# Routing the second layer in two groups of token tiles, with a memory region per expert, and splitting all its weights during the attention

## The reference: two layers of graph attention and experts over 1354 nodes

```
x = x + adj @ (layernorm(x) * W)                                   # layer 0, graph
h = layernorm(x); a = h + attention(layernorm(h), 8 heads)         # layer 0, block
x = x + a + moe0(layernorm(a))      # top 2 of 8 experts, the first 271 tokens of each
f = layernorm(x) @ Wg               # layer 1, graph
a1 = f @ attn_l; a2 = f @ attn_r
w = exp(leaky_relu(a1 + a2.T) - rowmax) * adj
x = x + elu((w / w.sum(1)) @ f)
t = layernorm(x)                    # layer 1, experts: no capacity limit
p = softmax(t @ Wg2 + bg); mask = top 2 of 8
x = x + sum_e (p * mask)[:, e] * (gelu(t @ W1[e] + b1[e]) @ W2[e] + b2[e])
```

## Time and profile before

| what | value |
|---|---|
| time, median of 3 runs | 944.22 us (939.36 to 947.76) |
| the profiled execution's own time | 947.76 us |
| its span, first to last instruction | 946.0 us |
| mean granted TensorE clock | 0.903 |
| busy: PE, DVE, ACT, POOL | 780.6, 599.7, 407.8, 313.5 us |
| fill of the scatter region of layer 1 (before) | 3842.5 KB in one transfer |
| split of the weights | 32 loads and 64 writes of 512 KB |

### The profile page before, as it was taken

The page is one execution under the profiler, slowest core; times in us unless marked ns, Lnnn a source line. Parts: engine busy times, 40 slices in busy tenths (PEclk is TensorE's granted clock), DMA queues, the critical chain, the costliest instruction groups (busy, mean ns, idle before and its releaser), DMA issues.

```text
span 946.0 us, 13697 instructions
## 1 busy us (share of the span) xinstructions
PE 780.6 (83%) x4168; PEld 591.3 (63%) x4169; DVE 599.7 (63%) x1174; ACT 407.8 (43%) x841; POOL 313.5 (33%) x329
## 2 busy tenths in 40 slices
PE   3978899999999998508799956599653999999993
PEld 3976555555555434407799954487532788888882
DVE  5665777766666756628888926696551565666662
ACT  3215435555556464504376633541500545444451
POOL 2000256666666761086400012000064223233221
PEclk9988979999999999757799987799656999999997
DMA  7698767787877662036544336450832168772223
GB/s 254 208 286 314 197 229 229 229 278 253 248 244 246 211 221 74 1 134 217 199 166 173 125 128 260 192 182 1 353 120 95 21 166 266 223 212 42 37 29 76
DMA packets 67217, 168.79 MB, mean 178 GB/s; under 512 B 20382, under 2 KB 45110, under 8 KB 64192
## 3 DMA queue, kind: packets, MB, share of 16 engines
q1 hardware_dynamic: 45664, 105.01, 33.5%
q0 software_dynamic: 21504, 63.17, 22.0%
HBM read 104.33 MB, written 58.90 MB: 173 GB/s over the span
## 4 chain that ended last, share of the span: by engine, by line
PE 71%; DVE 11%; issue 7%; DMA 4%; ACT 3%; POOL 2%; SPq 0%; POOLq 0%; DVEq 0%; ACTq 0%
PE ps L1182 11%; PE ps L1162 7%; PE ps L1174 5%; PE ps L1477 5%; PE ps L1393 4%; PE ps L1455 4%; PE ps L1288 3%; PE ps L1290 3%; PE ps L1289 3%; PE ps L1457 3%; PE ps L1456 3%; PE ps L1479 3%; PE ps L1464 3%; PE ps L1135 2%; DVE mx L1632 2%
## 5 line engine op out<-in xcount | busy, mean ns | idle before, releaser
L1632 DVE TENSOR_REDUCE mx<-ps 128x1 f32<-128x452 f32 x264 | 148.2, 622 | 66.0 <-PE ps L1162 65.1
L891 ACT ACTIVATE expo<-ps 128x452 f32<-128x452 f32 x264 | 124.5, 552 | 92.2 <-PE ps L1174 91.3
L1182 PE MATMUL ps<-expo,v_st 128*64 128x452 f32 (+1 forms) x576 | 117.7, 531 | 0.0
L1162 PE MATMUL ps<-k_st,q_st 96*128 96x452 f32 x264 | 106.7, 418 | 5.1 <-DVE mx L1632 4.7
L1056 ACT ACTIVATE h<-ps,b_l 128x128 f32<-128x128 f32 x232 | 63.0, 383 | 100.4 <-PE ps L1464 98.1
L1174 PE MATMUL ps<-q_st,k_st 98*128 98x452 f32 x264 | 96.8, 390 | 2.2 <-ACT expo L891 2.0
L828 POOL DMA_INDIRECT sum_d<-y1t,goal x29 | 46.3, 1596 | 140.3 <-DVE share L1975 113.8
L1477 PE MATMUL ps<-w_ring,h_hi 128*128 x232 | 83.1, 396 | 2.8 <-DVE y1t L2002 2.8
L1162 PEld LDWEIGHTS ps<-k_st,q_st 96*128 96x128 f32 x264 | 51.0, 193 | 52.2 <-DVE mx L1632 35.9
L1993 DVE COPY h1pre<-ps 128x1024 f32<-128x1024 f32 x29 | 35.5, 1225 | 72.7 <-PE ps L1457 72.7
L767 POOL TENSOR_TENSOR part_lo<-part,part_hi 128x512 fp32r<-128x512 f32 x56 | 70.8, 1290 | 0.4
(11 more groups left out here) (294 smaller groups left out, 1789.4 us busy)
## 6 DMA issues: line engine op xcount, KB each, us to landing
w_l<-w_l SPq DMA_DIRECT2D x8, 2053.0 KB, 8.7
part<-w_l POOLq DMA_DIRECT2D x32, 512.0 KB, 5.3
w_split_d<-part_lo POOLq DMA_DIRECT2D x32, 512.0 KB, 3.9
adj<-adj_t SPq DMA_DIRECT2D x22, 704.0 KB, 4.5
w_split_d<-part_hi POOLq DMA_DIRECT2D x28, 512.0 KB, 3.6
w_ring<-w_split_d SPq DMA_DIRECT2D x8, 1365.5 KB, 7.3
w_ring<-w_split_d SPq DMA_DIRECT2D x4, 1365.0 KB, 5.8
xs_d<-zeros SPq DMA_DIRECT2D x1, 3842.5 KB, 26.8
```

The lines of the kernel that those rows point to most:

```text
L891: act.activation(expo[g % 8][:, :], ps[:, 3 + g % 3, 0:QC], ACT.Exp, scale=SCALE).then_inc(s_exp, 1)
L1162: pe.matmul(ps[:, i % 3, 0:KC], q_st[h % 3][0:3 * DK, (n // KB) * P:(n // KB + 1) * P], k_st[h % 3][0:3 * DK, (n % KB) * KC:(n % KB + 1) * ...
L1182: return pe.matmul(ps[at:at + 2 * DK, 6 + g // T % 2, lo:hi], v_st[h % 2][:, kt, :], expo[g % 8][:, lo:hi], start=kt < 2, stop=kt == T - 1 ...
L1632: dve.tensor_reduce(mx4[:, n // KB, n % KB:n % KB + 1], ps[:, i % 3, 0:KC], AX_X, ALU.max).then_inc(s_mx, 1)
```

## The change

Seven edits go together.

- **Region per expert.** `xs1_d` has E regions of NP = 1408 rows (1060 bytes each) and one spare tile. The row number is the position plus a constant (`C_OFF1`), and the expert stage finds a tile's rows by a table `tile_row`, loaded into a register by POOL.
- **Fill.** The fill of `xs1_d` in the first stage shrinks to 128 rows; instead SP fills one expert's region (1408 rows) in each head.
- **Split.** All 32 parts are split in the attention; `choose` of layer 0 waits for all of them. The four late parts among the experts of layer 0 are gone.
- **Two groups.** Layer 1 is routed for tiles 0 to 7 (`route1(2, ...)`), then for 8 to 10 (`route1(3, ...)`). PE makes the kept products of tiles 8 and 9, turns and routes tiles 0 to 7, and then makes tile 10's. POOL scatters 16 times for the first group, then 6 times.
- **Scores apart.** The 2 score columns have products of their own into one bank, for a whole group, ahead of the features; ACT copies them once per group. The features have 256 columns and three banks. The features of tiles 8 to 10 come after the maximum.
- **Turned rows.** ACT copies both halves in the graph of layer 1; DVE none.
- **Adjacency rows.** SP issues the first three loads after all gathers.

```diff
-SLOTS1 = TILES1 * P
+SLOTS1 = E * NP + P
+    c[:, C_OFF1:C_OFF1 + E] = np.arange(E) * NP + 1
 # SP
-            sp.dma_start(xs1_d.rearrange("(k p) d -> p k d", p=P),
-                         zeros[:, None, :].to_broadcast([P, TILES1, ROW])).then_inc(s_zfill, 16)
+            sp.dma_start(xs1_d[E * NP:SLOTS1, :], zeros[:, :]).then_inc(s_zfill, 16)
...
                     if h + 1 < H:
                         load_values((h + 1) % 2, h + 1)
+                sp.dma_start(xs1_d[h * NP:(h + 1) * NP, :].rearrange("(k p) d -> p k d", p=P),
+                             zeros[:, None, :].to_broadcast([P, T, ROW])).then_inc(s_zfill, 16)
                 store_third(h, 0)
...
             sp.wait_ge(s_y0_ps, PRIMED + E)
+            for t in range(T):
+                sp.wait_ge(s_gath[t], 16)
             for j in range(3):
                 sp.dma_start(adj1[j][:, :], adj[j]).then_inc(s_adj1[j], 16)
-
-            for t in range(T):
-                sp.wait_ge(s_gath[t], 16)
 # POOL
-            split_parts(0, EARLY, part_hi)
-            pool.wait_ge(s_zfill, 48)
+            for n in range(PARTS1):
...
+            pool.wait_ge(s_zfill, 48 + 16 * E)
...
-            split_parts(EARLY, PARTS1, part_hi_late)
...
-            pool.wait_ge(s_norm_act, normed_act(5))
-            for n in range(2):
-                pool.wait_ge(s_idx, 2 + n)
-                for t in range(T):
-                    pool.indirect_dma_start(...)
+            for lo, hi, done in ((0, GA, 1), (GA, T, 3)):
+                for n in range(2):
+                    pool.wait_ge(s_idx, done + n + 1)
+                    for t in range(lo, hi):
+                        if n == 0:
+                            pool.wait_ge(s_norm_act, normed_act(5, t))
+                        pool.indirect_dma_start(...)
...
-                pool.dma_start(x1t[t % 3][:, :], xs1_d[t * P:(t + 1) * P, :]).then_inc(s_x1l[t % 3], 16)
+                row = pool.value_load(tile_row[0:1, t:t + 1], min_val=0, max_val=E * NP)
+                pool.dma_start(x1t[t % 3][:, :], xs1_d[bass.ds(row, P), :]).then_inc(s_x1l[t % 3], 16)
+            pool.wait_ge(s_te, 1)
 # ACT, graph of layer 1
             normed_group(0)
             turned_group(0)
+            column_scores(0)
+            features(0, 2, 0)
             normed_group(1)
-            features(0, 2)
+            features(2, 4, 0)
             turned_group(1)
-            features(2, 4)
+            column_scores(1)
+            features(4, 6, 1)
             normed_group(2)
-            features(4, 6)
+            features(6, 8, 1)
             turned_group(2)
-            features(6, T)
+            column_scores(2)
             act.wait_ge(s_am, 3)
             act.activation(fg[:, 0, :], agap[:, :], ACT.Exp)
             act.activation(fg[:, 1, :], agap[:, :], ACT.Exp, scale=0.2).then_inc(s_fg, 1)
+            features(8, T, 2)
...
+            def routed_group(n, lo, hi):
...
+                root_table()
+                raw_copies(3, lo, hi)
+                root_group(8 + n, lo, hi)
+                act.wait_ge(s_lg, 2 + n)
+                act.activation(probs[:, lo:hi, :], lg[:, lo:hi, :], ACT.Exp).then_inc(s_pexp, 1)
+                act.wait_ge(s_g1b, GB)
+                for t in range(lo, hi):
+                    act.activation(sent[:, t, 0:D], x_res[:, t, :], ACT.Identity, ...)
 # PE
+            column_scores(0)
             features(0)
             turn_group(1)
+            column_scores(1)
             features(1)
             turn_group(2)
             spread(0)
-            features(2)
+            column_scores(2)
             spread(1)
             pe.wait_ge(s_am, 1)
             pe.transpose(ps[0:1, 1, 0:P], a_max[:, :], ident).then_inc(s_small, 1)
             spread(2)
             pe.wait_ge(s_am, 2)
             pe.matmul(ps[:, 1, P:P + 1], ones[0:1, :], a_max1[:, :], ...)
+            features(2)
...
+            pe.wait_ge(s_z, GB)
+            rest(0)
+            rest(1)
+            pe.wait_ge(s_z, GA)
+            routed(0, GA, 1)
+            rest(2)
+            positions(2, 0, GA, 7)
+            pe.wait_ge(s_lg, 2)
+            routed(GA, T, 2)
+            positions(3, GA, T, 3)
+            pe.wait_ge(s_idx, 5)
 # DVE
             for k in range(2):
-                dve.wait_ge(s_lo_out[k], 16 * (EARLY // 2))
-            choose(0)
+                dve.wait_ge(s_lo_out[k], 16 * (PARTS1 // 2))
+            choose(1, 0, T)
...
+            def route1(k, lo, hi, bank):
...
+                choose(k, lo, hi)
+                dve.wait_ge(s_g1b, GB)
+                ...                                   # probs, comb: 5 steps
+                dve.wait_ge(s_pos, k)
+                ...                                   # slot, sa, sb_: 5 steps
+                row_number(sa, 0, lo, hi)
+                row_number(sb_, 1, lo, hi)
             settle(0, (0, GA), (0, GA))
-            elu(0, 0, GA)
+            step(elu(0, 0, GA))
+            route1(2, 0, GA, 7)
             dve.wait_ge(s_g1b, GB)
             settle(1, (0, GB), (GA, T))
             step(elu(1, GA, T))
-            inverse_root(mv[:, :, 1], rstd)
-            choose(1)
+            route1(3, GA, T, 3)
...                                                   # then the tables, with tile_row
```

More of the change, by code:

```diff
@@ L318, in tr_act_before @@
         def tr_act_before(r):
-            return sum(TR_BY_TILE.get(m, 3) for m in range(r))
+            return sum(6 if m == BY_ACT_HALVES else TR_BY_TILE.get(m, 3) for m in range(r))
         def tr_dve_before(r):
-            return sum(0 if m in TR_BY_TILE else 3 for m in range(r))
+            return sum(0 if m in TR_BY_TILE or m == BY_ACT_HALVES else 3 for m in range(r))
         def scratch(name, shape):
@@ L1404, in _, with rest @@
                     graph1(i * 3 + (2 + k), (2 + k) % 3, False)
[L1405 to L1406 removed]
+            def rest(t):
                 for j in range(T):
```

295 lines of the change are left out of this document (150 added, 145 removed).

## The result

| | kernel before | kernel after |
|---|---|---|
| time, median of 4 runs beside each other | 945.99 us (939.36 to 952.47) | 958.66 us (957.85 to 959.49) |
| ratio, 95% interval | | 1.0151 [1.0101, 1.0201] |
| span of the profiled execution | 946.0 us | 957.2 us |

The forecast was 941.5 us, no difference that can be told, and its range ended at 957. Slower by over 1% had a chance of 0.22. The two profiled spans lie 11.2 us apart, the forecast had them at -2.9. So 14.1 us are to be found.

What follows compares the result with a forecast made beforehand. PE was taken as busy for most of the span, with gains only where it waits. The terms +19 - 15.5 + 1.9 - 8.3 = -2.9 us gave, against 944.22, a forecast of 941.5 us, range 927 to 957.

Steps and rivals of the forecast that it cites:

- step 1: Attention: eight fills at 2.7 us each and four added parts end the split at 411.4; layer 0's routing starts 19 us late.
- step 5: Routing of layer 1: two groups start the scatters sooner, the ring's load stays hidden, b2 becomes the bound; -8.3 us.
- The rule of shared engines: Split in the attention: all queues share 16 DMA engines, so each fill costs its full 3.9 us, 31 instead of 21.6.
- Step 2: Experts 0 and 1 of layer 0: without the late splits beside them their stalls go; -15.5 us, bounds -5 and -17.
- Rival C: Experts 0 and 1 are slow for the cold clock, not POOL; step 2 gives only 3, time 954; chance 0.08.
- The port between DVE and POOL: Out projection: DVE's two-input additions and POOL's splits block each other; split perhaps 2 us later, sum 2 us worse.
- Step 3: Gather of layer 1: first gathers no longer run beside adjacency loads; -2.2 us at the first normalized tile.
- Step 4: Turning and features of layer 1: longer score columns offset by savings, taken as 0; then +1.9 us for copies before the exponentials.
- The last stage: Stage after the routing of layer 1: counted at no change, 0 us.
- B: Attention: fills delay POOL's loads and low writes more, slower by 1% at 4.2 us each, 960 at 5; chance 0.20.
- A: Attention: fills hide in POOL's computing time, 1 us each or less; time 928, or 922 if free; chance 0.27.
- D: Routing of layer 1: the first group's scatters start no earlier, step 5 gives 0, time 949.5; chance 0.10.

Runs made afterwards that it cites:

- run 8: Run 3's kernel, its last four parts loaded and written back but computed by POOL in one column only; ratio 0.7% below run 3.
- run 1: Kernel after with its eight fills moved from the attention heads to beside the experts of layer 0; 946.50 us against 946.93 for the kernel before.
- run 5: Kernel before plus, in each head, a fill of 1408 rows of a separate region, 28 parts still in the attention; 0.34% slower.
- run 3: Kernel before with all 32 parts split in the attention, nothing else changed; ratio 1.0019.
- run 2: Kernel after with the last four parts split among the experts of layer 0 again, fills still in the attention; 954.59 us.
- run 12: Run 9 with 28 parts in the attention and the last four among the experts of layer 0; 937.55 us against 936.88 for run 9.
- run 7: Run 1 with the kept products of tiles 8 to 10 made before tiles 0 to 7 are turned; layer-1 routing stage 63.8 us, whole time not given.
- run 9: Kernel after with fills beside layer 0's experts, the old feature stage and kept products first; 936.88 us against 944.51 for the kernel before.
- run 6: Run 1 with turning, score columns and features of the layer-1 graph as in the kernel before; ratio 0.9954 against 1.0018 for run 1.
- run 10: Run 1 with ACT copying the last features after the exponentials; feature stage 40.5 us against 40.8, whole time not given.
- run 4: Kernel before with only the layer-1 feature stage as in the kernel after (scores apart, ACT copies); 1.3% slower, stage 40.6 us instead of 34.9.
- run 11: Kernel before with the load of the ring's first half issued later, when the second row numbers are ready; ratio 1.0122.

## Why the prediction was wrong, step by step

Two steps missed by 4.7 us each. In step 1 only sizes were off; in step 5 the mechanism failed. No single step is the whole loss: with either of the two right, the span would have been 6.5 us longer than before instead of 11.2.

**Step 1, the split (+19, measured +23.7): mechanism right, two sizes off.** A fill costs 3.15 us in this pair, not 2.7 (+3.6 over eight). The queue share had led to 0.80 us per us, and I then took 0.7 "since some of the 38.6 us will be other things": with 0.8 the sum would have been right. The rule of shared engines gave 31 (the Trainium skill, DMA: Bandwidth & Descriptors, as cited in the prediction), against 25.2 measured: not all of a fill's estimated time is paid. Four parts took 29.5 us, not 27.9. The pace of 6.97 was read from three casts, and the fourth of the kernel before stands 9.4 us behind the third. In the six runs with 32 parts and no fills, the four take 29.2 to 34.0 us, and 31.6 in run 8, where POOL hardly computes: so their transfers set the pace there. That context rows of the out projection slow them is likely but not shown. Run 1 and run 5 show the fill's share, both ways.

**Step 2, experts 0 and 1 (-15.5, measured -16.5): right.** Run 3 and run 2 tie it to the four parts. The size was read from one execution, though, the longest of the six (run 3, above): typically it is 10. And run 12 shows that by the whole time nothing can be told between the two places of the four parts, since what the experts win is lost before the routing. Rival C is dead.

**The port between DVE and POOL.** I had put 2 us on the split for it. It did not hit the split but the out projection, where it stretches DVE's additions from 0.62 to 1.1 to 1.6 us (runs 3 and 8). The Trainium skill (SBUF — State Buffer, "Who interferes with whom") names just such a pair, a DVE instruction with two SBUF inputs and a GpSimd instruction that reads SBUF, and here the traces agree. With the fills gone the out projection is what ends last: the variance is ready at 393.1, 398.0, 400.0, 401.8 and 404.2 us in the five runs (7, 9, 6, 10, 1) that are the same kernel up to there, and at 391.5 to 393.1 in the four (the kernel before, 4, 11, 12) that split 28 parts without fills. The spread has several parts. Runs 7 and 1 are 11.1 us apart: 3.1 before the first of the nine additions, 5.1 in the additions themselves, and the other 2.9 in waits between and behind them, mostly for PE's products. Both, busy by stretch (PE, PEld, DVE, ACT, POOL, PEclk, DMA share, GB/s):

```profile
378.00:384.00 6.00, 5.76 (x23) 4.34 (x23) 5.71 (x11) 0.57 (x2) 4.68 (x6) 0.66 0.69 238
384.00:390.00 6.00, 5.88 (x38) 5.19 (x38) 2.96 (x12) 1.35 (x4) 4.41 (x5) 1.00 0.39 138
```
```profile
378.00:384.00 6.00, 6.00 (x24) 5.39 (x23) 4.18 (x4) 1.15 (x3) 4.91 (x6) 0.50 0.62 202
384.00:390.00 6.00, 2.80 (x7) 1.69 (x5) 5.93 (x4) 0.00 (x0) 4.66 (x5) 0.50 0.62 226
```

In run 1 PE waited 5.03 us for DVE, worked at a granted clock of 0.50 from 378 on, waited 4.42 us more behind an addition of 3.11 us, and so does 7 products in 6 us where run 7 does 38 at 1.00. Step 1's sentence "out projection and layernorm before it are hidden by that wait and cost nothing" holds for the kernel after, but this is why removing the fills gives 11 us there (16 in the mean of the five) and not the 25 that they cost the split.

**Step 3, gather (-2.2, measured -1.9): right.**

**Step 4, features (0 with step 3, measured +4.6; then 1.9 of it for the copies): mis-sized.** The score columns took 6.9 us for 6.2. I had also taken off 1.0 us of waits of PE for the copies, but the waits shrank by 0.2 only (0.78 + 0.45 + 0.74 us after, 0.87 + 0.83 + 0.46 before). And the second group's features take 1.7 us more, the first group's 0.35 less. That comes to some 2.9 us too good, where gather and features together missed by 2.7. Runs 4 and 6 give 5.1 to 5.7 us for the stage, in both directions.

**Step 5, routing of layer 1 (-8.3, measured -3.6): this is the step that failed.** The sentence was "The first half of the ring is issued at 680.6 and takes 23.0, to 703.6: hidden, with 11 us left". The time of issue was right (30.9 us behind the first kept product, forecast and measured), and hidden was right for the load itself, which landed after 24.9 us in run 1. What I did not ask is whom it runs beside. In the kernel before it landed 1 us before the first scatter. The change brings the scatters forward and the load back, and so puts the two on top of each other. Run 7 takes them apart for the most part and the stage reaches -9.3; run 11 puts them together in the kernel before and costs 7.

The sentence "The bound is now b2, not the scatters" fell with it. Counted from the first kept product, the first rows were to be there after 60.8 us and the last `b2` addition after 64.7. In the five profiles with this order (after, runs 1, 2, 6, 10) the rows are there after 66.7 to 69.8 us; in the four runs `b2` ends after 60.1 to 63.2, and PE waits for a DMA. So `b2` was counted 1.5 to 4.6 us too long and the rows 5.9 to 9.0 us too short. Only the later of the two counts, so the stage missed by 2 to 5 us and not by 6 to 9. (The prediction's 710.5 for the rows is not its own sum either: 698.9 + 7.7 + 2.4 + 2.7 is 711.7. Nothing rests on it.)

The kernel after is the mixed case. In its profiled execution the first rows and the last `b2` addition are both there after 69.2 to 69.3 us; `b2` had been held up by the 5.81 us in the chain above. By these times the rows alone would have set nearly the same start without that stall. Whether that stall on DVE has the same cause stays open: run 1 has the same overlap and not this stall.

**The last stage (0, measured +3.0).** From its first turned rows to its first scatter it takes 25.8 us instead of 24.1, with a granted clock of 0.53 over its first 9 us where the kernel before had 0.73. The other 1.4 us lie between its first and last scatter (190.0 us and 188.6), where runs 3, 4, 5, 8 and 11, which do not touch this stage, have 188.4 to 190.1. In whole, this stage takes 223.0 to 225.5 us in the runs built on the kernel before and 222.6 to 228.4 in those built on the kernel after, so a part of the 3.0 may be spread between executions. I have no experiment on it.

**Rivals.** B had the right sign and the right place, but at 3.15 us a fill it alone gives about zero, as its own threshold (3.0) says: the loss needed steps 4 and 5 as well. A (fills hide) and D (first scatters no earlier) are refuted: the first scatter comes 11.1 us sooner behind the first kept product (29.5 and 40.6).

## What to carry to other kernels

A transfer that lands in time is not free: look at what else is on the engines between its issue and its landing, and above all whether the change moves a latency-bound chain of small scatters into that stretch. Two edits that each fit into one reserve must be costed together; here 2.5 and 7.6 us in single profiles became 23.7, and in time the fills cost 3 us with 28 parts and 12.6 with 32. And a gain read as the end of a stall should be taken from several executions, since one profile can stand at the long end.

## What the runs showed that I had not expected

- A zero fill of 1.49 MB (an estimated 3.9 us at 387 GB/s) lands after 11.3 us beside the split and delays it by 2.6 to 4.4 us, 3.3 in the mean; beside the experts of layer 0 the same eight fills cost nothing that can be told.
- Scatters of 128 rows land in 2.7 us in the median behind the load of 8.4 MB and in 15.9 us beside it (run 11), and that load itself grows from 23.1 to 24.2 us only: nearly all of it is paid by the small transfers.
- One and the same instruction list reached the same point of layer 0 at 393 to 404 us. Between the two ends, DVE additions stretched by POOL's instructions are the largest part, 5.1 us, and products at a granted clock of 0.50 another.
